# Local attention: sums of squares as four 64x64 tiles, rotation re-split between three engines, exponentials kept in PSUM

## The chip, the cores and the metric

The kernel runs on one core of one Trainium2 chip. The metric is the device time of one execution in microseconds. Before the change the median of two runs was 2688.89 us (2684.29 and 2693.5).

## What is computed

The reference is a stack of four layers on an input of 8 x 256 positions with 128 channels: additive attention, six blocks of local attention with a gated feed-forward part, a state-space layer, and a mixture of eight experts. The change touches only the second, which takes three quarters of the time. Per block, cut to what matters:

```
qkv = x @ Wqkv                                  # 16 heads of 64
q = q / max(norm(q), 1e-12) * q_scale           # norm over the 64 of a head
k = k / max(norm(k), 1e-12) * k_scale
q = q*cos*scale + rotate_half(q)*sin*scale      # rotary, per position
k = k*cos/scale + rotate_half(k)*sin/scale
sim = q . k over a window of 32 and the one before, * 8, masked
attn = softmax(sim);  out = attn @ v;  x = x + out @ Wo
x = x + (a * gelu(gate)) @ W2                   # (a, gate) = layernorm(x) @ W1
```

## The kernel before

`local_attention` (line 296 on) cuts the 2048 positions into four units of 512. Six layers of four units give 24 units, numbered i. Each unit has eight slots, j = 0 to 7, one for each pair of heads. The loop over the units 1 to 22 is a hardware loop (line 354); unit 0, unit 23 and the tail are written out. The order of the work on each engine is written out by hand, in a function `slot` per engine, and all engines meet through semaphores that count.

What slot j of unit i does is a pipeline. A pair of heads is projected in one slot, normalised in the next and scored in the one after:

- PE (TensorE), from line 528: scores of pair j (a mask by L449, then 32 small matmuls by L456), projection of q and k of pair j+2 (L429, L430, into PSUM banks 0 and 1), v of pair j+2 (L417, bank 2), the product of attention and v of pair j-2 (L477, bank 7), transposes of the probabilities of pair j-1 (L465, bank 6), and the sums of squares of pair j+2 (`norms`, L435 and L436, again into banks 0 and 1). `norms` multiplies 128 x 1024 squares by a 128 x 128 matrix that is block-diagonal, one 64 x 64 block of ones for each head of the pair.
- ACT (ScalarE), from line 642: a copy of the projection to SBUF (`f_raw`, L606), its square (L609), the exponential of the scores in place in SBUF (L662), copies of v (L598) and of the attention output (L634), three copies that spread the transposed probabilities (L624 to L627), and ln and exp for the inverse norm (L615, L617).
- POOL (GpSimd): `f_raw` times the cosine table (L707), then the sum of both halves of the rotation (L711).
- DVE (VectorE), from line 790: maximum and shift of the scores of pair j (L763, L767), normalisation of pair j+1 into `f_qk` (L755), the partition shuffle of `f_raw` of pair j+2 (L745), that times the sine table (L748), then the sum, the reciprocal and the scaling of the probabilities of pair j (L774, L776, L778).

The work behind the attention of unit i-1 is spread over the slots of unit i. On PE: `Wo` in slots 0 to 2 (L490, six, six and four passes), the mean of the layer norm in slot 3 (L497), its variance in slot 4 (L503), the gate and hidden matmuls in slots 5 to 7 (L510, L517), `W2` in slot 7 (L524). On DVE: the residual sum and `shift_in` of the new y into `f_xs2` at the end of slot 2 (L813, L724, L726), the centring at the end of slot 3 (L818, L821), the product with the inverse deviation at the end of slot 4 (L825), `shift_in` of the next unit's input at the end of slot 5, three `hidden` products (L786) in slots 6, 6 and 7. On ACT: square, ln and exp of the layer norm in slot 4 (L657, L676, L678), scale and bias in slot 5 (L667), three gelus with a table load before and after them (L639, L652) at the slots' border 5/6.

"Slot start" below is the start of L449, the mask of the scores. A float32 matmul appears as two records.

## Time and profile before

| | us |
|---|---|
| median of the runs shown | 2688.89 |
| the profiled execution, its own time | 2695.59 |
| its span in the profile | 2693.8 |
| PE busy | 2427.3 (90%) |
| DVE busy | 2276.3 (85%) |
| ACT busy | 1801.3 (67%) |
| POOL busy | 1082.1 (40%) |
| mean granted TensorE clock | 0.962 of 2.4 GHz |

The 192 slots of the local attention lie between 97 and 2150 us of the span. The time before them is additive attention; behind them come the state space and the experts, which the change leaves alone. A busy PE in the profile is not PE at its peak: records of matmuls overlap, so the pace of PE is read from the starts of successive groups.

### The profile page before, as it was taken

What the parts mean: (1) busy time and instruction counts of PE and PEld (TensorE: products, weight loads), DVE (VectorE), ACT (ScalarE), POOL (GpSimd) and SP (SyncE); (2) the same over time, 40 slices, a digit from 0 to 9 for tenths busy, and PEclk for the clock granted to TensorE, in tenths of its full rate; (3) what the DMA queues carried; (4) which work ended last, traced back from release to release, by engine and by line L of the source; (5) the groups of instructions that cost most, each with busy time, mean ns of one, the idle gap of its engine ahead of it and who ended that gap; (6) DMA issues with size and microseconds to landing.
All of it is one profiled execution on the core that took longest, in us unless ns stands there. A gap on an engine that the chain in (4) does not pass through costs nothing. (4 is left out here: it accounts for less than half of the span.)

```text
span 2693.8 us, 62735 instructions
## 1 busy us (share of the span) xinstructions
PE 2427.3 (90%) x24940; PEld 1267.8 (47%) x24940; DVE 2276.3 (85%) x2595; ACT 1801.3 (67%) x2593; POOL 1082.1 (40%) x461
## 2 busy tenths in 40 slices
PE   7899999999999999999999999999999977767778
PEld 2355555445555555455555555455545522222355
DVE  5799998998899998999889988998889848999542
ACT  4667776777677766777667766677677656545533
...
GB/s 20 53 2 2 2 25 10 10 2 1 14 22 10 2 2 13 14 18 1 2 14 14 15 5 2 13 14 9 10 2 2 2 36 0 0 0 0 18 16 47
DMA packets 16016, 29.85 MB, mean 11 GB/s; under 512 B 3616, under 2 KB 6064, under 8 KB 15664
## 3 DMA queue, kind: packets, MB, share of 16 engines
...
HBM read 24.73 MB, written 1.05 MB: 10 GB/s over the span
## 5 line engine op out<-in xcount | busy, mean ns | idle before, releaser
L707 POOL TENSOR_TENSOR f_rot<-f_raw,f_tabc 128x1024 f32<-128x1024 f32 x192 | 453.8, 2364 | 993.6 <-DVE f_qk L755 448.6
L711 POOL TENSOR_TENSOR f_rot<-f_rot,f_shuf 128x1024 f32<-128x1024 f32 x192 | 452.0, 2354 | 235.5 <-DVE f_shuf L748 235.5
L606 ACT ACTIVATE f_raw<-f_ps 128x1024 f32<-128x1024 f32 x192 | 196.1, 1021 | 348.6 <-PE f_ps L430 348.6
L748 DVE TENSOR_TENSOR f_shuf<-f_shuf,f_tabs 128x1024 f32<-128x1024 f32 x192 | 417.9, 2177 | 8.7
L778 DVE TENSOR_TENSOR f_s<-f_s,f_rcp 128x512 f32<-128x512 f32 x192 | 401.0, 2089 | 6.6
L477 PEld LDWEIGHTS f_ps<-f_ptz,f_v 64*64 64x64 f32 x6144 | 259.5, 133 | 96.0 <-issue 96.0
L477 PE MATMUL f_ps<-f_ptz,f_v 64*64 64x96 f32 (+1 forms) x6144 | 285.9, 243 | 1.9 <-ACT f_ptz L627 1.7
L429 PE MATMUL f_ps<-f_xs,f_wq 128*128 128x512 f32 x384 | 225.2, 670 | 46.9 <-DVE f_xs L726 34.6
L745 DVE STREAM_SHUFFLE f_shuf<-f_raw 128x1024 f32<-128x1024 f32 x192 | 257.7, 1342 | 0.6
L755 DVE SCALAR_TENSOR_TENSOR f_qk<-f_rn,f_rot 128x1024 f32<-128x1024 f32 x192 | 233.0, 1214 | 2.5 <-POOL f_rot L711 2.5
L456 PE MATMUL f_ps<-f_qk 64*32 64x64 f32 x12288 | 198.8, 220 | 34.8 <-issue 34.8
L615 ACT ACTIVATE f_rn<-f_ps 128x1024 f32<-128x1024 f32 x192 | 198.3, 1033 | 46.0 <-PE f_ps L436 45.6
L617 ACT ACTIVATE f_rn<-f_rn,k_lift 128x1024 f32<-128x1024 f32 x192 | 220.5, 1149 | 6.3
L417 PE MATMUL f_ps<-f_wv,f_xs 128*64 128x256 f32 x1536 | 216.3, 404 | 0.0
L430 PE MATMUL f_ps<-f_xs,f_wk 128*128 128x512 f32 x384 | 210.3, 631 | 0.0
L1133 POOL TENSOR_TENSOR s_prod<-s_state,s_cs 128x1024 f32<-128x1024 f32 x64 | 151.7, 2371 | 145.5 <-DVE s_state L1211 145.5
L609 ACT ACTIVATE f_sq<-f_raw 128x1024 f32<-128x1024 f32 x192 | 203.1, 1058 | 6.1
L435 PE MATMUL f_ps<-f_sq,f_same 128*128 128x512 f32 x384 | 197.7, 597 | 5.9 <-ACT f_sq L609 5.9
L456 PEld LDWEIGHTS f_ps<-f_qk 64*32 64x32 f32 x12288 | 163.5, 106 | 78.7 <-issue 78.7
L436 PE MATMUL f_ps<-f_sq,f_same 128*128 128x512 f32 x384 | 197.0, 595 | 0.0
L490 PE MATMUL f_ps<-f_o,f_wo 128*128 128x512 f32 x384 | 183.8, 612 | 0.0
L417 PEld LDWEIGHTS f_ps<-f_wv,f_xs 128*64 128x64 f32 x1536 | 96.1, 140 | 172.3 <-issue 144.1
...
## 6 DMA issues: line engine op xcount, KB each, us to landing
...
```

The lines of the kernel that those rows point to most:

```text
L417: mm = pe.matmul(view(ps, 2 * CH + 256 * r, [1, 256], p0=64 * h, rows=64), xs[:, at:at + 64], view(wv, CH * (q // 4) + 64 * h, [128, 4], [ ...
L429: pe.matmul(bank(0), wq[:, 128 * j:128 * j + 128], xs[:, :], start=True, stop=True)
L430: pe.matmul(bank(1), wk[:, 128 * j:128 * j + 128], xs[:, :], start=True, stop=True).then_inc(sem["a_mm"], 1)
L456: mm = pe.matmul(view(ps, (4 + h) * CH + (w // 4) * 64, [1, 64], p0=WIN * (w % 4), rows=WIN), t[64 * h:64 * h + 64, WIN * w:WIN * w + WIN] ...
L477: mm = pe.matmul(view(ps, 7 * CH + 64 * p, [1, n], p0=64 * h, rows=64), v[64 * h:64 * h + 64, p * CH + 64 * j:p * CH + 64 * j + 64], ptz[6 ...
L617: act.activation(rn[:, :], rn[:, :], ACT.Exp, scale=-0.5, bias=con.lift).then_inc(sem["rn"], 1)
L707: pool.tensor_tensor(view(rot, 0, [S, 4], [1, S]), view(raw, 0, [S, 4], [1, S]), view(tab_c, 0, [S, 2], [0, 2], [1, S]), ALU.mult).then_in ...
L711: pool.tensor_tensor(rot[:, :], rot[:, :], shuf[:, :], ALU.add).then_inc(sem["rot"], 1)
L745: dve.stream_shuffle(shuf[:, :], raw[:, :], [(p + 16) % 32 for p in range(32)]).then_inc(sem["shuf"], 1)
L748: dve.tensor_tensor(view(shuf, 0, [S, 4], [1, S]), view(shuf, 0, [S, 4], [1, S]), view(tab_s, 0, [S, 2], [0, 2], [1, S]), ALU.mult).then_i ...
L755: dve.scalar_tensor_tensor(out=view(qk[j % 2], 0, [KOFF, 2], [1, UNIT]), in0=view(rn, 0, [UNIT, 2], [1, UNIT]), scalar=1e12, in1=view(rot, ...
L778: dve.tensor_tensor(view(t, 0, [64, 8], [1, 64]), view(t, 0, [64, 8], [1, 64]), view(rc, 0, [1, 8], [0, 64]), ALU.mult).then_inc(sem["p"], 1)
```

## The change

Projection weights are rearranged on the host so that bank 0 holds q of the pair's first head in partitions 0 to 63 and k of the second head in 64 to 127, and bank 1 the other two. ACT no longer copies the projection to `f_raw`. It squares it straight from PSUM in four activations of 64 partitions, two of which write the squares of k to the other half of the partitions (`f_cross`). `norms` becomes four matmuls with a 64 x 64 matrix of ones, one for each quarter of the array, into banks 6 and 7 instead of 0 and 1. DVE shuffles the projection from PSUM and multiplies it, also from PSUM, with the cosine table; POOL now multiplies the shuffled copy with the sine table and adds. The exponentials are written to PSUM over the scores (banks 4 and 5), and the DVE sums and scales them from there. v moves to bank 6, the transposes to bank 2, the variance to bank 3, the first gate matmul to bank 6. SP's weight loads keep their order, in another loop.

In program order: ACT does the exponential of a slot ahead of the squares, where it came after `f_raw` and its square; DVE does shuffle and cosine product behind the scaling of the probabilities, where shuffle and sine product came ahead of it. `norms` waits for the squares, the copy of v and the copy of the attention output (`f_o`); scores wait for the scaled probabilities of the pair before (`f_p`) instead of for their shift.

```
-    GBANK = (2, 0, 1)
+    GBANK = (6, 0, 1)
+    NBANK = (6, 7)
 def project(i, j):                                   # PE
-    need(pe, sem["ln"], i * 8 + j)
+    need(pe, sem["sq"], i * 8 + j)
+    need(pe, sem["shuf"], i * 8 + j)
+    need(pe, sem["straight"], i * 8 + j)
 def norms(i, j):                                     # PE
-    need(pe, sem["sq"], i * 8 + j + 1)
-    pe.matmul(bank(0), same_head[:, :], sq[:, 0:UNIT], start=True, stop=True)
-    pe.matmul(bank(1), same_head[:, :], sq[:, UNIT:], start=True, stop=True).then_inc(sem["n_mm"], 1)
+    gather(sem["sq"], i * 8 + j + 1)
+    gather(sem["v"], i * 8 + j + 1)
+    gather(sem["o"], i * 8 + j - 3)
+    for own in (True, False):
+        for h in range(2):
+            k = slice(64 * h, 64 * h + 64)
+            of = sq[k, UNIT * h:UNIT * h + UNIT] if own else cross[k, :]
+            mm = pe.matmul(view(ps, NBANK[h] * CH, [1, CH], p0=64 * (h if own else 1 - h), rows=64),
+                           same_head[k, k], of, start=True, stop=True, skip_group_check=True)
+    mm.then_inc(sem["n_mm"], 1)
 def scores(i, j):                                    # PE
-    gather(sem["shift"], i * 8 + j)
+    gather(sem["p"], i * 8 + j)
 def square(i, j):                                    # ACT, for raw_copy
+    for own in (False, True):
+        for h in range(2):
+            k, other = slice(64 * h, 64 * h + 64), slice(64 * (1 - h), 64 * (1 - h) + 64)
+            to = sq[k, UNIT * h:UNIT * h + UNIT] if own else cross[other, :]
+            ins = act.activation(to, view(ps, (h if own else 1 - h) * CH, [1, CH], p0=64 * h, rows=64), ACT.Square)
+    ins.then_inc(sem["sq"], 1)
 def rotate(i, j):                                    # POOL
+    pool.tensor_tensor(shuf, shuf, tab_s, ALU.mult).then_inc(sem["turned"], 1)
     pool.tensor_tensor(rot[:, :], rot[:, :], shuf[:, :], ALU.add).then_inc(sem["rot"], 1)
 def shuffle(i, j):                                   # DVE
+    need(dve, sem["sq"], i * 8 + j + 1)
+    dve.stream_shuffle(shuf[:, :], view(ps, 0, [1, 2 * CH]), [(p + 16) % 32 for p in range(32)])
 def straight(i, j):                                  # DVE
+    dve.tensor_tensor(rot, ps banks 0 and 1, tab_c, ALU.mult).then_inc(sem["straight"], 1)
 def soft_b(i, j):                                    # DVE
-    dve.tensor_tensor(s, s, rc, ALU.mult)            # all three in SBUF
+    dve.tensor_tensor(s, ps banks 4 and 5, rc, ALU.mult)
 def gate_mm / hid_mm: hid_mm(k, 0) now comes ahead of gate_mm(k, 0), which waits for "ln" of the slot
```

ACT in slot 5 of the looped unit. Before (`f_cen`, `f_xn` and the second `f_sq` belong to the layer norm of the unit before):

```order
L678 ACTIVATE f_sq<-f_sq 128x512 [waits f_ln2]
L292 REGISTER_ALU
L606 ACTIVATE f_raw<-f_ps 128x1024 [waits f_straight,f_shuf,f_a_mm]
L609 ACTIVATE f_sq<-f_raw 128x1024 [waits f_n_mm,f_raw]
L598 ACTIVATE f_v<-f_ps 128x2x256 [waits f_v_mm]
L662 ACTIVATE f_s<-f_s 128x512 [waits f_shift]
L667 ACTIVATE f_xn<-f_xn,f_fcol 128x512 [waits f_scaled]
L634 ACTIVATE f_o<-f_ps 128x512 [waits f_pv_mm]
```

and now:

```order
L722 ACTIVATE f_sq<-f_sq 128x512 [waits f_ln2]
L700 ACTIVATE f_ps<-f_s 128x2x256 [waits f_shift]
L292 REGISTER_ALU
L652 ACTIVATE f_cross<-f_ps 64x512 [waits f_n_mm,f_a_mm]
L652 ACTIVATE f_cross<-f_ps 64x512
L652 ACTIVATE f_sq<-f_ps 64x512 x2
L641 ACTIVATE f_v<-f_ps 128x2x256 [waits f_v_mm]
L711 ACTIVATE f_xn<-f_xn,f_fcol 128x512 [waits f_scaled]
L679 ACTIVATE f_o<-f_ps 128x512 [waits f_pv_mm]
```

The exponential (`f_s`, waiting for `f_shift`) has moved from behind the squares to ahead of them.

PE from the transposes of slot 5 to the scores of slot 6. Before:

```order
L465 MATMUL f_ps<-f_ident,f_s 128x128 x3
L292 REGISTER_ALU
L435 MATMUL f_ps<-f_sq,f_same 128x512 [waits f_sq]
L436 MATMUL f_ps<-f_sq,f_same 128x512
L510 MATMUL f_ps<-f_xn,f_w 128x512 [waits f_w1,f_xn,f_v]
L517 MATMUL f_ps<-f_xn,f_w 128x512
L449 MATMUL f_ps<-f_maskb,f_identb 128x256 [waits f_qk,f_shift]
```

and now:

```order
L507 MATMUL f_ps<-f_ident,f_s 128x128 x3
L435 REGISTER_ALU
L475 MATMUL f_ps<-f_sq,f_same 64x512 [waits f_sq,f_v,f_o]
L475 MATMUL f_ps<-f_sq,f_same 64x512
L475 MATMUL f_ps<-f_cross,f_same 64x512 x2
L558 MATMUL f_ps<-f_xn,f_w 128x512 [waits f_w1,f_xn]
L548 MATMUL f_ps<-f_xn,f_w 128x512 [waits f_ln]
L490 MATMUL f_ps<-f_maskb,f_identb 128x256 [waits f_qk,f_p]
```

The sums of squares wait for two more results, the gate matmul for the ln that reads them, and the scores for the scaled probabilities.

DVE around the end of slot 4. Before:

```order
L755 SCALAR_TENSOR_TENSOR f_qk<-f_rn,f_rot 128x2x512 [waits f_rn,f_rot]
L292 REGISTER_ALU
L745 STREAM_SHUFFLE f_shuf<-f_raw 128x1024 [waits f_raw,f_rot]
L748 TENSOR_TENSOR f_shuf<-f_shuf,f_tabs 128x1024 [waits f_tab,f_shuf]
L774 TENSOR_REDUCE f_sum<-f_s 128x8 [waits f_exp]
L776 RECIPROCAL f_rcp<-f_sum 128x8 [waits f_sum]
L778 TENSOR_TENSOR f_s<-f_s,f_rcp 128x512 [waits f_rcp]
L825 TENSOR_TENSOR f_xn<-f_cen,f_sq 128x512 [waits f_fcol,f_rs2]
L763 TENSOR_REDUCE f_max<-f_ps 128x8 [waits f_s_mm]
```

and now:

```order
L802 SCALAR_TENSOR_TENSOR f_qk<-f_rn,f_rot 128x2x512 [waits f_rn,f_rot]
L822 TENSOR_REDUCE f_sum<-f_ps 128x8 [waits f_exp]
L825 RECIPROCAL f_rcp<-f_sum 128x8 [waits f_sum]
L827 TENSOR_TENSOR f_s<-f_ps,f_rcp 128x2x4x64 [waits f_rcp]
L292 REGISTER_ALU
L788 STREAM_SHUFFLE f_shuf<-f_ps 128x1024 [waits f_sq,f_rot]
L795 TENSOR_TENSOR f_rot<-f_ps,f_tabc 128x1024 [waits f_qk,f_tab,f_sq]
L875 TENSOR_TENSOR f_xn<-f_cen,f_sq 128x512 [waits f_fcol,f_rs2]
L811 TENSOR_REDUCE f_max<-f_ps 128x8 [waits f_s_mm]
```

The product into `f_xn` stays last in the slot and ahead of the next slot's maximum; in front of it stand now the shuffle and the cosine product, which read PSUM, and the shuffle waits for the squares.

## Rows read from the trace of the kernel before

**Rows 1.** Timeline of PE, slot 3: start us, us, operation, xcount
```profile
1238.82 0.38 PE L449 MATMUL f_ps<-f_maskb,f_identb 128*128 128x256 bf16 x2
...
1242.08 1.08 PE L417 MATMUL f_ps<-f_wv,f_xs 128*64 128x256 f32 x8
1243.09 1.49 PE L477 MATMUL f_ps<-f_ptz,f_v 64*64 64x96 f32 x32
1244.51 1.13 PE L497 MATMUL f_ps<-f_xs,k_ones 128*128 128x512 f32 x2
...
1245.91 1.02 PE L435 MATMUL f_ps<-f_sq,f_same 128*128 128x512 f32 x2
...
1247.63 0.38 PE L449 MATMUL f_ps<-f_maskb,f_identb 128*128 128x256 bf16 x2
```

**Rows 2.** Timeline of PE, slots 5 to 0: idle time before in brackets
```profile
1256.85 0.38 PE L449 MATMUL f_ps<-f_maskb,f_identb 128*128 128x256 bf16 x2
...
1265.89 1.10 PE L510 MATMUL f_ps<-f_xn,f_w 128*128 128x512 f32 x2 [0.84 <-issue]
...
1267.68 0.38 PE L449 MATMUL f_ps<-f_maskb,f_identb 128*128 128x256 bf16 x2
...
1273.52 1.12 PE L429 MATMUL f_ps<-f_xs,f_wq 128*128 128x512 f32 x2 [1.20 <-DVE f_xs L726]
...
1279.56 0.38 PE L449 MATMUL f_ps<-f_maskb,f_identb 128*128 128x256 bf16 x2
...
1291.40 0.38 PE L449 MATMUL f_ps<-f_maskb,f_identb 128*128 128x256 bf16 x2 [0.43 <-issue]
...
1294.60 0.64 PE L456 MATMUL f_ps<-f_qk 64*32 64x64 f32 x11 [2.04 <-issue]
```

**Rows 3.** Windows: most of the stage, two slots 0; length, engines' busy times, PEclk
```profile
130.00:2130.00 2000.00, 1890.83 (x22806) 1023.99 (x22806) 1812.51 (x2087) 1438.26 (x2088) 878.12 (x373) 0.98 0.03 9
1206.32:1218.80 12.48, 10.72 (x125) 5.85 (x126) 12.09 (x14) 5.17 (x9) 6.83 (x3) 1.00 0.06 18
1291.40:1306.85 15.45, 13.41 (x124) 6.78 (x125) 12.83 (x14) 5.20 (x9) 7.06 (x3) 0.78 0.01 2
```

**Rows 4.** Timeline of DVE and POOL, slots 3 and 4
```profile
1243.48 0.69 DVE L763 TENSOR_REDUCE f_max<-f_ps 128x8 f32<-128x512 f32 x1
...
1244.82 1.22 DVE L755 SCALAR_TENSOR_TENSOR f_qk<-f_rn,f_rot 128x1024 f32<-128x1024 f32 x1
...
1245.96 1.33 DVE L745 STREAM_SHUFFLE f_shuf<-f_raw 128x1024 f32<-128x1024 f32 x1
1246.20 2.36 POOL L707 TENSOR_TENSOR f_rot<-f_raw,f_tabc 128x1024 f32<-128x1024 f32 x1 [4.86 <-DVE f_qk L755]
...
1247.32 2.33 DVE L748 TENSOR_TENSOR f_shuf<-f_shuf,f_tabs 128x1024 f32<-128x1024 f32 x1
...
1249.79 2.35 POOL L711 TENSOR_TENSOR f_rot<-f_rot,f_shuf 128x1024 f32<-128x1024 f32 x1 [1.23 <-DVE f_shuf L748]
...
1250.52 2.18 DVE L778 TENSOR_TENSOR f_s<-f_s,f_rcp 128x512 f32<-128x512 f32 x1
```

**Rows 5.** The line of `shift_in`: durations ns min/median/max, first and last start us, forms
```profile
L724 DVE TENSOR_SCALAR f_xs<-y_t x48: 407/416/421, 80.4 to 2159.9; 64x512 f32 x44, 64x512 f32<-64x512 f32 x4
```

**Rows 6.** Timeline of ACT, slots 3 to 5
```profile
1242.19 1.02 ACT L606 ACTIVATE f_raw<-f_ps 128x1024 f32<-128x1024 f32 x1 [0.96 <-PE f_ps L430]
...
1245.47 0.58 ACT L598 ACTIVATE f_v<-f_ps 128x512 f32<-128x512 f32 x1
1245.95 0.59 ACT L634 ACTIVATE f_o<-f_ps 128x512 f32<-128x512 f32 x1
...
1257.16 1.05 ACT L615 ACTIVATE f_rn<-f_ps 128x1024 f32<-128x1024 f32 x1
...
1260.00 0.63 ACT L678 ACTIVATE f_sq<-f_sq 128x512 f32<-128x512 f32 x1
1260.54 1.00 ACT L606 ACTIVATE f_raw<-f_ps 128x1024 f32<-128x1024 f32 x1
...
1264.46 0.63 ACT L662 ACTIVATE f_s<-f_s 128x512 f32<-128x512 f32 x1 [1.34 <-DVE f_s L767]
```

More of the change, by code:

```diff
@@ L321, in local_attention @@
         v = m.sb("f_v", 8 * CH)
[L322 to L324 removed]
+        sq, shuf, rot = (m.sb(f"f_{n}", 2 * UNIT) for n in ("sq", "shuf", "rot"))
+        rn, cross = m.sb("f_rn", 2 * UNIT), m.sb("f_cross", UNIT)
+        AT = (WIN, 2 * WIN + UNIT)
+        qk = [m.sb(f"f_qk{b}", AT[1] + UNIT) for b in range(2)]
         s = [m.sb(f"f_s{b}", UNIT) for b in range(2)]
@@ L378, in weights, with load_w1, load_w2, layer @@
             sp.dma_start(wo[:, :], io["f_wo"][r]).then_inc(sem["wo"], 16)
-            need(sp, sem["h_mm"], t * 3)
+        def load_w1(sp, r, t):
+            gather(sp, sem["h_mm"], t * 3)
             sp.dma_start(w1[:, :], io["f_w1"][r]).then_inc(sem["w1"], 16)
-            need(sp, sem["w2_mm"], t)
+        def load_w2(sp, r, t):
+            gather(sp, sem["w2_mm"], t)
             sp.dma_start(w2[:, :], io["f_w2"][r]).then_inc(sem["w2"], 16)
+        def layer(sp, r, first, last):
+            for q in range(8 * NU):
+                if not first and q == 4:
+                    load_wo(sp, r, r * NU)
+                if not first and q == 9:
+                    load_w1(sp, r, r * NU)
+                if not first and q == 10:
+                    load_w2(sp, r, r * NU)
+                if not last and q == 8 * NU - 5:
+                    load_qkv(sp, r + 1, (r + 1) * NU, 0)
+                if not last and q == 8 * NU - 1:
+                    load_qkv(sp, r + 1, (r + 1) * NU, 1)
@@ L392, in _ @@
             load(sp, sem["const"], consts)
-            weights(sp, 0, 0)
-            with sp.Fori(1, DEPTH) as r:
-                weights(sp, r, r * NU)
+            for k in range(2):
+                load_qkv(sp, 0, 0, k)
+            load_wo(sp, 0, 0)
+            load_w1(sp, 0, 0)
+            load_w2(sp, 0, 0)
+            layer(sp, 0, True, False)
+            with sp.Fori(1, DEPTH - 1) as r:
+                layer(sp, r, False, False)
+            layer(sp, DEPTH - 1, False, True)
         @block.tensor
@@ L652, in slot @@
                     nc.scalar.preload_act_table_set(ACT_SET)
+                if run:
+                    need(act, sem["shift"], i * 8 + j + 1)
+                    act.activation(view(ps, 4 * CH, [CH, 2], [64, 4], [1, 64]), view(s[j % 2], 0, [64, 2], [128, 4], [1, 64]),
+                                   ACT.Exp, scale=8.0).then_inc(sem["exp"], 1)
                 if has:
-                    raw_copy(u, a)
+                    square(u, a)
                 if before and j == 4:
@@ L657, in slot @@
                     act.activation(sq2[:, :], cen[:, :], ACT.Square).then_inc(sem["sq2"], 1)
-                if has and j == 5:
-                    value_copy(u, a)
-                if run:
-                    need(act, sem["shift"], i * 8 + j + 1)
-                    act.activation(s[j % 2][:, :], s[j % 2][:, :], ACT.Exp, scale=8.0).then_inc(sem["exp"], 1)
-                if has and j != 5:
+                if has:
                     value_copy(u, a)
@@ L675, in slot @@
                     need(act, sem["var"], k + 1)
-                    act.activation(sq2[:, :], bank(2), ACT.Ln, bias=con.eps).then_inc(sem["ln2"], 1)
+                    act.activation(sq2[:, :], bank(3), ACT.Ln, bias=con.eps).then_inc(sem["ln2"], 1)
                     need(act, sem["ln2"], k + 1)
@@ L810, in slot @@
                     soft_b(i, j)
+                if has:
+                    shuffle(u, a)
+                    straight(u, a)
                 if before and j == 2:
```

134 lines of the change are left out of this document (71 added, 63 removed).

## Prediction

> **What bounds the kernel now.** I read the shares of busy time first, then the starts of groups on PE through one unit, then what PE waited for, and then DVE, POOL and ACT in the same stretch. The starts on PE show one slot of local attention as a closed row of groups: slot 3 goes from 1238.82 to 1247.63, 8.81 us, with no idle time given [rows 1]. The sums of squares take 1247.63 - 1245.91 = 1.72 us of it, four records of 0.43 us. Slot 5 takes 10.83 us, slot 6 11.88, slot 7 11.84, and in these PE waits 0.84, 1.20 and 0.43 us [rows 2]. Slot 0 takes 12.48 us at full clock and 15.45 where the granted clock is 0.78 (a part of it at 1.2 instead of 2.4 GHz), and PE stands idle for 2.04 us inside the scores [rows 2, 3]. So PE sets the pace with few waits, some 86 us per unit.
>
> DVE is nearly as full, but part of its time is standing behind POOL. The product L748 begins at 1247.32 and ends at 1249.65, that is 1.09 us after POOL's L707 ended (1246.20 + 2.36 = 1248.56). L778 begins at 1250.52 and ends at 1252.70, 0.56 us after L711 ended (1252.14). Both read two tensors from SBUF, as POOL does. The shuffle L745, with one, takes its 1.33 us right beside L707 [rows 4].
>
> **The change, part by part.** I count in microseconds from the slot's start, and price slots 0 to 7 of a looped unit.
>
> PE, sums of squares. Before, two 128x128 matmuls of 512 columns, 1.72 us. Now four 64x64 tiles. v's matmuls (128x64, two tiles) bring eight records of 256 columns, 0.215 each in sequence, 1.72 together, into 1243.09 - 1242.08 = 1.01 us [rows 1]: two tiles run beside each other (0.86) and the change of array shape costs 0.15. If all four tiles run together the new sums cost two passes of 0.43, plus about 0.25 for two changes of shape: 1.1 us, 0.62 less. If only two do, it is 1.72 + 0.25, 0.25 more. Tiles that share rows do overlap in v's rows, so I take four: -0.62 wherever PE alone sets the slot.
>
> DVE. The sine product (2.33) becomes a cosine product from PSUM. The nearest row, the shift, is 512 columns from PSUM in 0.69, so some 1.2 for 1024; the scaling (2.18) becomes 0.7. That frees 2.6 us a slot, but of the chain to `f_qk` nothing gets shorter. POOL now starts only behind the shuffle and does both of its operations in a row. The cycle is shuffle 1.36, POOL 2.36 + 2.35 with 0.2 of semaphores, normalisation 1.14, sum to scaling 1.6: 9.0 us [rows 4]. That is under the mean slot of 10.6 ((1291.40 - 1206.32) / 8 [rows 2, 3]), above PE's new slot 3; it hides over the unit as a whole.
>
> ACT. Copy and square (2.1 us) become four activations of 64 partitions; 512 columns follow each other at 1245.95 - 1245.47 = 0.48 [rows 6], so 1.95. Nothing gained. But the exponential now stands ahead of them, and `norms` waits for the copy of the attention output, which is third behind them. That is a new chain: DVE's shift of slot j, exponential (0.65), squares (1.95), v (0.5), output (0.6), sums of squares on PE. Before, the squares started 1242.19 - 1238.82 = 3.37 into the slot whatever DVE did [rows 6]. Where the shift ends 2.7 into the slot, as without extra work on DVE, the sums start at 6.6 instead of 6.1. Where it is late, PE now waits for it.
>
> Slots 0 and 1: six `Wo` passes (2.6) cover the new wait. -0.6 each. Slot 2: the squares start 1.8 later, behind `Wo`; sums at 8.15 against 7.9: -0.4.
>
> Slot 3: DVE's shuffle of slot 2 started at 7.0. Behind it come the cosine product, the residual sum and three instructions of `shift_in`. These used to run with POOL idle; now POOL's product runs until 10.8. One bound is that they are not held: shift of slot 3 ends at 3.3, PE does slot 3 in 8.2 (-0.6). The other is that they are held as L748 and L778 are, and again by the sum behind it: DVE is free 5.0 into slot 3, shift 6.3, squares until 8.9, sums at 9.95, slot 11.0 (+2.2). No row shows this kind beside POOL; its 512 columns take 0.416 [rows 5], faster than the 0.69 of every form that runs undisturbed, so I take it as held once: shift ends at 3.9, slot 8.5, -0.3.
>
> Slot 4: the centring, behind the cosine product, ends about 3.6 into the slot, the shift at 5.0, squares 7.6, the layer norm's own square, v and output 9.15, sums until 10.1, variance: 11.1 instead of 9.23, +1.9 (9.5 with nothing held, 10.1 in a long slot 3).
>
> Slot 5: the inverse deviation comes from ACT behind ln and exp of the norm. That sequence took from 1257.16 to 1260.63, 3.47 us [rows 6]; it now starts when slot 4's sums are done, and ends 2.7 into slot 5. DVE then does `f_xn`, two tensors from SBUF with POOL's sum running: held, like L778, until about 3.9. Shift 5.2, exponential 5.9, squares 7.9, v, `f_xn`'s bias 0.75, output: 9.6; sums until 10.6; then the first hidden matmul, and the gate matmul behind the ln: 13.2 instead of 10.83, +2.4. Before, the exponential stood just as late (1264.46, 7.6 into the slot) and it hurt nothing, because raw copy and square had gone first (1260.54) [rows 2, 6]. Even with nothing held I get 12.75, +1.9. This is the surest loss.
>
> Slot 6: `f_xs` comes earlier, PE's 1.20 goes; next is `hidden`, now ahead of the scaling that the scores wait for: 11.1, -0.7. Slot 7: -0.4, with a wait of 0.3 for the output copy.
>
> Sum of a unit: -0.6 - 0.6 - 0.4 - 0.3 + 1.9 + 2.4 - 0.7 - 0.4 = +1.3, to which the clock comes. The mean clock of 0.98 [rows 3] means 4% of the time, 3.5 us per unit, at 1.2 GHz, and it follows idle time of some 2.5 us around slot 0. In slot 0, (1 - 0.78) x 2 x 15.45 = 6.8 us at half clock cost 15.45 - 12.48 = 3.0, 0.44 per us. The new waits of PE (3 in slot 4, 3.5 in slot 5) are as long as that. With as much half clock once more per unit, 3.5 x 0.44 = 1.5. Zero and 4 are the ends.
>
> So +2.8 per unit, for 23 units, and nothing for unit 0, which has no feed-forward work: +64. On the profiled execution's 2695.6 (span 2693.8) that is 2760; the median shown is 6.7 lower, so 2753. SP's weight loads keep their order and conditions: 0.
>
> On the port the Trainium skill (SBUF — State Buffer, section on the two sides of SBUF) says that DVE operations in a 2-port mode or with two SBUF inputs and GpSimd's operations exclude each other for a whole instruction. Rows 4 agree for two inputs. By that rule `shift_in` is held as well, which is the long slot 3 below.
>
> **The rivals.** (a) *Held twice.* POOL's sum gets the port between two instructions of `shift_in`. Slots 3, 4, 5 are 11.0, 10.1, 12.95: +5.2 instead of +4.0. With a clock loss of up to 4: +6.5 x 23 = +150 at worst, about 2805 with middle values. For it: the two holds in rows 4. Against: DVE may keep its turn.
> (b) *Nothing held but `f_xn`, clock unchanged.* Slots 3 to 5 come to 31.8 against 28.9, +2.9, the others -2.7: +0.2, 2695.
> (c) *PE's saving stands: faster.* The place is the start of the sums in slot 5, the price 0.62 a slot. If they start before 7.0, and in slot 4 before 7.2, the waits are covered: -0.6 in each of slots 0, 1, 3 and 4, -0.4 in 2 and 7, -0.7 in 6, 0 in 5, together -3.9 x 23 = -90, so 2600. For it: DVE really loses 2.6 us a slot, and with the cover of slot 0 everything could run earlier than my chain says. Against: the 3.47 us on ACT are no shorter.
> (d) *Tiles run two by two.* +0.87 in the PE-bound slots 0, 1, 2, 7: +3.5 more per unit, 2830.
>
> On tiles that share a bank the Trainium skill (TensorEngine Tiling (Array Packing), Gotcha 1) says that different row tiles can't write the same PSUM bank at once. Here each row half writes its own bank, 6 or 7. The rule speaks for four at a time, as the sum has it.
>
> **How the numbers follow.** The forecast 0.42, (a) 0.20, (b) 0.18, (c) 0.15, (d) 0.05. A measurement here can tell about 2%, 54 us, from no change: slower is above 2743. The forecast lies just above, so I give 0.25 of its 0.42 to slower and 0.17 to the same. Slower 0.50, same 0.35, faster 0.15. The range goes from 2635, inside the gap to (c), to 2835.
>
> **What would show it.** Right: in the rows of PE, slots 4 and 5 longer than 9.23 and 10.83 with idle time ahead of the sums, named after `f_o`; the sums taking 1.0 to 1.2 us; DVE's products at 1.2 and 0.7 us; DVE busy far less and idle behind POOL; a product into `f_xn` of over 0.7 us; the granted clock below 0.98. Wrong: sums in slot 5 starting right behind the transposes, slots of 10.2 or less there, or half-clock stretches around slot 0 alone.

## The result and the profile after

The changed kernel takes 2788.86 us (median of two runs, 2788.75 and 2788.98) against 2688.89. The ratio is 1.037, 95% interval 1.033 to 1.041: slower. The profiled execution took 2788.98 us with a span of 2787.2, and that is 93.4 us more than the span of before. The forecast was 2753 and slower.

The busy times first. This is part 1 of the page, and two rows of its part 5 (busy, mean ns of one, then the idle time ahead of them and who ended it):

```profile
PE 2354.2 (84%) x25708; PEld 1190.9 (43%) x25708; DVE 1980.3 (71%) x2597; ACT 1898.5 (68%) x2977; POOL 1081.4 (39%) x461
...
L475 PE MATMUL f_ps<-f_sq,f_same 64*64 64x512 f32 x768 | 218.6, 641 | 264.6 <-ACT f_o L679 255.6
...
L802 DVE SCALAR_TENSOR_TENSOR f_qk<-f_rn,f_rot 128x1024 f32<-128x1024 f32 x192 | 233.9, 1218 | 70.4 <-POOL f_rot L754 70.0
```

PE has 73 us less to do and DVE 296 us less, and yet the kernel is longer: PE now stands for 264.6 us ahead of the sums of squares, nearly all of it for the copy of the attention output, `f_o`. The timeline of PE shows where. These are the sums at the end of slot 0, then slots 3 to 7 and the next slot 0, in the looped unit that begins at 1174 (start us, us, idle time in brackets; L490 is the mask that starts a slot, L475 the sums of squares):

```profile
1183.23 0.65 PE L475 MATMUL f_ps<-f_sq,f_same 64*64 64x512 f32 x2
...
1183.72 0.60 PE L475 MATMUL f_ps<-f_cross,f_same 64*64 64x512 f32 x2
1184.25 0.39 PE L490 MATMUL f_ps<-f_maskb,f_identb 128*128 128x256 bf16 x2
...
1203.73 0.39 PE L490 MATMUL f_ps<-f_maskb,f_identb 128*128 128x256 bf16 x2
...
1214.02 0.65 PE L475 MATMUL f_ps<-f_sq,f_same 64*64 64x512 f32 x2 [3.13 <-ACT f_o L679]
...
1215.04 0.39 PE L490 MATMUL f_ps<-f_maskb,f_identb 128*128 128x256 bf16 x2
...
1223.63 0.65 PE L475 MATMUL f_ps<-f_sq,f_same 64*64 64x512 f32 x2 [2.34 <-ACT f_o L679]
...
1225.61 0.38 PE L490 MATMUL f_ps<-f_maskb,f_identb 128*128 128x256 bf16 x2
...
1235.28 0.65 PE L475 MATMUL f_ps<-f_sq,f_same 64*64 64x512 f32 x2 [3.43 <-ACT f_o L679]
...
1236.30 2.08 PE L558 MATMUL f_ps<-f_xn,f_w 128*128 128x512 f32 x2
1238.17 1.80 PE L548 MATMUL f_ps<-f_xn,f_w 128*128 128x512 f32 x2
1239.81 0.38 PE L490 MATMUL f_ps<-f_maskb,f_identb 128*128 128x256 bf16 x2
...
1251.07 0.39 PE L490 MATMUL f_ps<-f_maskb,f_identb 128*128 128x256 bf16 x2
1259.06 0.65 PE L475 MATMUL f_ps<-f_sq,f_same 64*64 64x512 f32 x2 [0.82 <-ACT f_o L679]
1263.69 0.38 PE L490 MATMUL f_ps<-f_maskb,f_identb 128*128 128x256 bf16 x2 [0.77 <-issue]
...
1273.73 0.39 PE L490 MATMUL f_ps<-f_maskb,f_identb 128*128 128x256 bf16 x2
```

The rows of the four tiles start 0.49 us apart, and the scores' mask follows after 1184.25 - 1183.23 = 1.02 us, where it followed 1.72 us after the start of two full ones [rows 1]. So the tiles do what they should. But slot 3 is 11.31 us (8.81 in rows 1), slot 4 10.57, slot 5 14.20 (10.83 in rows 2). The slots of all looped units, from the starts of the scores' mask, as medians over 22 units:

| slot | 0 | 1 | 2 | 3 | 4 | 5 | 6 | 7 | mean unit |
|---|---|---|---|---|---|---|---|---|---|
| before | 14.0 | 10.5 | 9.5 | 8.8 | 9.2 | 10.8 | 11.8 | 11.9 | 86.4 |
| after | 10.0 | 9.8 | 9.7 | 11.3 | 11.0 | 14.2 | 11.3 | 12.3 | 89.9 |

Of the 93.4 us, 78 lie in the 22 looped units (3.55 each). Unit 0 is 3.2 us longer and unit 23, up to its last slot, 6.2, and the first slot starts at 105.1 us instead of 98.1, though nothing ahead of it was meant to change; why it does was not looked into. The windows that answer to [rows 3], the same stretch and slots 3, 4, 5 and 0 of the unit above (length, busy PE, PEld, DVE, ACT, POOL, granted clock, DMA share, GB/s):

```profile
130.00:2130.00 2000.00, 1739.87 (x22657) 908.85 (x22656) 1467.76 (x2005) 1470.81 (x2361) 843.62 (x358) 0.96 0.03 8
...
1203.73:1215.04 11.31, 8.18 (x128) 4.49 (x125) 10.57 (x14) 7.20 (x12) 4.71 (x3) 1.00 0.01 1
1215.04:1225.61 10.57, 8.23 (x128) 4.51 (x125) 8.62 (x12) 8.66 (x14) 6.31 (x3) 1.00 0.01 2
1225.61:1239.81 14.20, 10.77 (x128) 5.38 (x127) 10.88 (x12) 11.60 (x18) 7.16 (x4) 0.88 0.01 1
...
1263.69:1273.73 10.04, 9.85 (x129) 5.21 (x129) 7.12 (x11) 4.99 (x11) 5.69 (x3) 1.00 0.09 23
```

The clock of 0.96 instead of 0.98 means about (1 - 0.96) x 2 x 2000 = 160 us at 1.2 GHz instead of 80. Per looped unit the clock records give 7.0 us at 1.2 GHz instead of 3.6. Before, all of it lay in slot 0; now there is none there, and 2.9 lie in slot 4 and 3.6 in slot 5. In the unit above the clock fell after idle stretches of 3.13, 2.34 and 3.43 us, and the two feed-forward groups at the end of slot 5 take 1.87 and 1.64 us in place of about 0.9 each [rows 2]. Slot 0, on the other hand, has lost its stop: 10.04 us at full clock, against 12.48 and 15.45 [rows 3].

Why the sums come late in slot 3 is seen on DVE, POOL and ACT from the end of slot 2 to the end of slot 3; this answers to [rows 4, 6]:

```profile
1202.86 1.21 DVE L795 TENSOR_TENSOR f_rot<-f_ps,f_tabc 128x1024 f32<-128x1024 f32 x1
...
1204.70 0.99 DVE L767 TENSOR_SCALAR f_xs<-y_t 64x512 f32 x1
1205.70 2.56 DVE L769 TENSOR_SCALAR f_xs<-y_t 64x255 f32 x2
...
1209.02 0.69 DVE L815 TENSOR_TENSOR f_s<-f_ps,f_max 128x512 f32<-128x512 f32 x1
...
1211.71 0.69 DVE L827 TENSOR_TENSOR f_s<-f_ps,f_rcp 128x512 f32<-128x512 f32 x1
```

```profile
1203.04 2.36 POOL L750 TENSOR_TENSOR f_shuf<-f_shuf,f_tabs 128x1024 f32<-128x1024 f32 x1 [6.25 <-DVE f_shuf L788]
1205.55 2.35 POOL L754 TENSOR_TENSOR f_rot<-f_rot,f_shuf 128x1024 f32<-128x1024 f32 x1
```

```profile
1209.74 0.60 ACT L700 ACTIVATE f_ps<-f_s 128x512 f32<-128x512 f32 x1 [3.67 <-DVE f_s L815]
1210.37 1.19 ACT L652 ACTIVATE f_cross<-f_ps 64x512 f32<-64x512 f32 x2
1211.57 1.19 ACT L652 ACTIVATE f_sq<-f_ps 64x512 f32<-64x512 f32 x2
1212.79 0.60 ACT L641 ACTIVATE f_v<-f_ps 128x512 f32<-128x512 f32 x1
1213.28 0.59 ACT L679 ACTIVATE f_o<-f_ps 128x512 f32<-128x512 f32 x1
```

Read it from below. PE's sums start at 1214.02, when `f_o` is written; it is behind v, the four squares (2.4 us) and the exponential, and ACT stood idle for 3.67 us because DVE's shift ended at 1209.71. DVE was in `shift_in`: its first copy, 0.41 to 0.42 us when undisturbed [rows 5], ends at 1205.69 behind POOL's product (ends 1205.40), the second pair takes 2.56 us and ends at 1208.26 behind POOL's sum (ends 1207.90).

### The profile page after: what moved, and what is told of

Read it like the earlier page. It is cut to its first block and busy times, and to the rows that moved or that the text cites. A ratio compares the mean times of both kernels' runs of the same rounds, so it can differ in the third digit from the quotient of the medians.

```text
span 2787.2 us, 65659 instructions
## 1 busy us (share of the span) xinstructions
PE 2354.2 (84%) x25708; PEld 1190.9 (43%) x25708; DVE 1980.3 (71%) x2597; ACT 1898.5 (68%) x2977; POOL 1081.4 (39%) x461
## 5 line engine op out<-in xcount | busy, mean ns | idle before, releaser
L750 POOL TENSOR_TENSOR f_shuf<-f_shuf,f_tabs 128x1024 f32<-128x1024 f32 x192 | 452.6, 2357 | 1293.0 <-DVE f_shuf L788 1293.0
L475 PE MATMUL f_ps<-f_sq,f_same 64*64 64x512 f32 x768 | 218.6, 641 | 264.6 <-ACT f_o L679 255.6
L700 ACT ACTIVATE f_ps<-f_s 128x512 f32<-128x512 f32 x192 | 115.6, 602 | 279.6 <-DVE f_s L815 279.4
L652 ACT ACTIVATE f_cross<-f_ps 64x512 f32<-64x512 f32 x384 | 226.9, 591 | 91.7 <-PE f_ps L464 86.4
L788 DVE STREAM_SHUFFLE f_shuf<-f_ps 128x1024 f32<-128x1024 f32 x192 | 249.9, 1302 | 0.9
L811 DVE TENSOR_REDUCE f_max<-f_ps 128x8 f32<-128x512 f32 x192 | 131.9, 687 | 154.8 <-PE f_ps L498 153.3
L795 DVE TENSOR_TENSOR f_rot<-f_ps,f_tabc 128x1024 f32<-128x1024 f32 x192 | 231.5, 1206 | 0.0
L652 ACT ACTIVATE f_sq<-f_ps 64x512 f32<-64x512 f32 x384 | 227.0, 591 | 4.5
L475 PE MATMUL f_ps<-f_cross,f_same 64*64 64x512 f32 x768 | 218.8, 648 | 0.0
L449 PE MATMUL f_ps<-f_wv,f_xs 128*64 128x256 f32 x1536 | 210.4, 395 | 1.2 <-ACT f_rn L659 1.2
```

Source lines behind the costliest of these rows:

```text
L449: mm = pe.matmul(view(ps, 6 * CH + 256 * r, [1, 256], p0=64 * h, rows=64), xs[:, at:at + 64], view(wv, CH * (q // 4) + 64 * h, [128, 4], [ ...
L475: mm = pe.matmul(view(ps, NBANK[h] * CH, [1, CH], p0=64 * (h if own else 1 - h), rows=64), same_head[k, k], of, start=True, stop=True, ski ...
L652: ins = act.activation(to, view(ps, (h if own else 1 - h) * CH, [1, CH], p0=64 * h, rows=64), ACT.Square)
L750: pool.tensor_tensor(view(shuf, 0, [S, 4], [1, S]), view(shuf, 0, [S, 4], [1, S]), view(tab_s, 0, [S, 2], [0, 2], [1, S]), ALU.mult).then_ ...
L788: dve.stream_shuffle(shuf[:, :], view(ps, 0, [1, 2 * CH]), [(p + 16) % 32 for p in range(32)]).then_inc(sem["shuf"], 1)
L795: dve.tensor_tensor(view(rot, 0, [S, 4], [1, S]), view(ps, 0, [S, 4], [1, S]), view(tab_c, 0, [S, 2], [0, 2], [1, S]), ALU.mult).then_inc( ...
```

## The experiments

The first six start from the changed kernel, the last four from the kernel before. The ratio is to the kernel before, measured beside each; a gain is counted from the changed kernel's 2788.86 us. "Slots" are medians as in the table, and times into a slot are medians over the looped units too.

**1. Undoing the order of ScalarE in slots 3 to 5.**

```
-                if run:
+                if run and j not in (3, 4, 5):
                     (exponential, ahead of the squares)
+                if run and j in (3, 4, 5):
+                    (the same, behind the copy to f_o)
```

> The changed kernel, with the exponential of slots 3, 4 and 5 moved behind squares, copy of v and output copy on ACT. Theory, the new wait of the sums is the exponential ahead of the squares: the sums start 7 us into the slot whatever DVE does; slots 3, 4, 5 go from 11.3, 11.0, 14.1 to about 9, 9.4, 11.3, together 7 us per unit, about 2630 us. Rival, DVE's lateness itself sets the slot, because the scores wait for the scaled probabilities that come out of the same chain: the three slots lose under 2 us together, 2745 or more.

Measured: 2720.35 us, ratio 1.010 (1.006 to 1.014), between the two expectations. Slots 3 to 7: 9.1, 10.8, 12.0, 12.4, 12.3. Of the 98 us that separate the changed kernel from the kernel before (2690.41 beside this run), 68 go. Slots 3 and 5 lose 2.2 us each, slot 4 little and slot 6 gets longer by 1.1. The PE rows of slot 4 show what comes in its place:

```profile
1087.13 0.38 PE L490 MATMUL f_ps<-f_maskb,f_identb 128*128 128x256 bf16 x2 [0.93 <-DVE f_s L831]
1089.47 1.10 PE L463 MATMUL f_ps<-f_xs,f_wq 128*128 128x512 f32 x2 [1.04 <-DVE f_rot L799]
1095.78 0.65 PE L475 MATMUL f_ps<-f_sq,f_same 64*64 64x512 f32 x2 [1.33 <-ACT f_o L679]
```

The late exponential makes the scaled probabilities and the rotation late, and the scores and the projection of the next slot wait for them.

**2. The product with the inverse deviation one slot later on DVE, behind the maximum and shift of slot 5.**

```
                 if run:
                     soft_a(i, j)
+                if before and j == 5:
+                    need(dve, sem["rs2"], k + 1)
+                    need(dve, sem["fcol"], k + 1)
+                    dve.tensor_tensor(xn[:, :], cen[:, :], sq2[:, :], ALU.mult)...
-                if before and j == 4:      (the same, at the end of slot 4)
```

> The changed kernel, with the product into f_xn moved on DVE from the end of slot 4 to behind maximum and shift of slot 5. Theory, the wait for the inverse deviation (f_rs2) delays the shift of slot 5 and with it all on ACT: the shift of slot 5 ends at 2.7 instead of 4.4 us, the sums start at about 7.3 instead of 9.7, slot 5 falls from 14.1 to about 11; 3 us per unit, about 2720 us. Rival, the gate matmul's wait for ln or the half clock sets slot 5: it loses under 1 us, 2765 or more.

Measured: 2720.26 us, ratio 1.010 (1.007 to 1.014). Slot 5 falls from 14.2 to 11.0, no other by more than 0.2; slot 3 rises by 0.4. A hit. The wait of DVE for ACT's ln and exp stood ahead of the shift of slot 5, and with it the whole chain. In the changed kernel the row is:

```profile
1228.25 0.69 DVE L875 TENSOR_TENSOR f_xn<-f_cen,f_sq 128x512 f32<-128x512 f32 x1 [3.89 <-ACT f_sq L722]
```

Of the 3.2 us, 1.9 are sums that start earlier (7.8 us into the slot instead of 9.7); the other 1.3 are the end of the slot, which has no half clock any more.

**3. `shift_in` and the copy to `f_fcol` with the factor 1 read from a column in SBUF instead of a constant.**

```
-  dve.tensor_scalar(to[0:64, :], y[...], 1.0, None, ALU.mult)
+  dve.tensor_scalar(to[0:64, :], y[...], one[0:64, 0:1], None, ALU.mult)      (and the three others)
```

> The changed kernel, with the 1.0 of shift_in and of the copy into f_fcol read from a column of ones instead of given as a constant (L736 in the kernel before has that form and takes 1.35 ns per element, longer than shift_in's 0.8). Theory, held at the port: this form waits for nobody on POOL; the three instructions take 0.6 + 0.35 + 0.35 instead of 0.99 + 2.56 us, f_fcol 0.15 instead of 1.45. Slot 3 falls from 11.3 to about 8.8 us, slot 4 from 11.0 to about 10.3; 3.3 us per unit, about 2713 us. Rival, the sums of squares are late for another reason (the order on ACT alone): shift_in gets shorter and slots 3 and 4 lose under 0.5 us each, 2770 or more.

Measured: 2804.08 us, 1.040 (1.036 to 1.044). A miss: this form is held all the same, and slot 3 is 11.7.

```profile
1208.18 0.99 DVE L768 TENSOR_SCALAR f_xs<-y_t,f_one 64x512 f32 x1
1209.18 2.62 DVE L770 TENSOR_SCALAR f_xs<-y_t,f_one 64x255 f32 x2
```

So it says nothing on what the hold costs. Edits 2 and 3 together:

> Both edits of the two runs before: plain form of shift_in, product into f_xn behind the shift of slot 5. Theory, two separate delays: the gains add, about 6.3 us per unit, 2645 us, below the kernel before. Rival, one takes the place of the other: no faster than the better of the two alone.

2718.07 us, 1.009 (1.006 to 1.012), slots 3 to 5 11.9, 11.1, 11.0: edit 2 alone, within 3 us.

**4. The same copies as the larger of a value and itself, two operands in SBUF.**

```
-  dve.tensor_scalar(to[0:64, :], y[...], 1.0, None, ALU.mult)
+  dve.tensor_tensor(to[0:64, :], y[...], y[...], ALU.max)                    (and the three others)
```

> The changed kernel, with the copies of shift_in and of f_fcol written as products of two operands in SBUF (the larger of a value and itself) in place of a multiplication by a number: the form of f_xn's product, which the trace doesn't show held by POOL. Theory (the hold by POOL delays DVE's shift of slot 3, behind it the exponential, the squares and PE's sums): the three copies take about 0.5, 0.5 and 0.2 us instead of 0.99, 2.56 and 1.45; slot 3 falls from 11.3 to 8.8 to 9.3 us, slot 4 from 11.0 to 10.3 or stays, slot 5 keeps its 14.1; 23 times about 3 us: 2715 to 2735 us. Rival (slot 3 is long because the exponential stands ahead of the squares, and the hold only comes in its shadow): slot 3 stays above 10.5 us, 2770 to 2790 us.

Measured: 2813.17 us, 1.045 (1.043 to 1.048). Both expectations missed, but the miss is worth more than a hit:

```profile
1213.83 1.25 DVE L767 TENSOR_TENSOR f_xs<-y_t 64x512 f32 x1
1215.10 2.82 DVE L769 TENSOR_TENSOR f_xs<-y_t 64x255 f32 x2
```

The copies are held too and take 0.5 us longer (4.07 in place of 3.55 us), and slot 3 is 12.4 instead of 11.3, 1.1 more where DVE shows 0.5. A longer hold makes a longer slot 3: PE's sums start 10.8 us into it instead of 10.3. Most of the rest is the clock: the sums themselves take 1.5 us instead of 1.1, and slot 3 has 1.2 us at half clock on average, where the changed kernel has 0.35. With edit 2 on top:

> The changed kernel with both edits: the copies in the two-operand form, and f_xn's product behind soft_a of slot 5. If the two losses are separate, slots 3, 4, 5 are about 9.1, 10.5 and 11.0 us (they were 11.3, 11.0, 14.1), and the time is that of the later product alone, 2720 us, less what the form gives by itself, 55 to 75 us: 2645 to 2665 us, below the kernel before. If they share one wait (PE late in slot 3 also makes slot 5 late), less than the sum: 2680 to 2720 us.

2735.84 us, 1.018 (1.015 to 1.020), slots 3 to 5 12.7, 11.1, 11.0: 77 us less than with the copies alone. Both ranges missed, since the shorter slot 3 that they counted on did not come. The later product is worth 69 us on the changed kernel, 86 on the copies of edit 3 and 77 here, and slot 5 comes to 11.0 each time, however long slot 3 is; the two losses are separate.

**5. `f_xs` formed from PSUM.** The three instructions add y and the bank of the output projection themselves, ahead of y's own sum:

```
-  dve.tensor_tensor(ycol, ycol, bank(3), ALU.add)
-  need(dve, sem["y1"], k + 1)
-  shift_in(xs2, k % NU, sem["xs2"])
-  need(pe, sem["xs2"], i + 1)                (ahead of the mean's matmul)
+  need(pe, sem["y1"], i + 1)
+  dve.tensor_tensor(xs2[0:64, :], y[0:64, ...], bank(3)[0:64, :], ALU.add)
+  for b in range(2):
+      mm = dve.tensor_tensor(xs2[64:128, ...], y[64:128, ...], bank(3)[64:128, ...], ALU.add)
+  mm.then_inc(sem["xs2"], 1)
+  need(dve, sem["xs2"], k + 1)
+  dve.tensor_tensor(ycol, ycol, bank(3), ALU.add)
```

> The changed kernel, with f_xs for the mean formed at slot 2 straight from y and the bank of the output projection (three sums with one operand in PSUM, 64x512 and twice 64x255) ahead of y's own sum, in place of copies from y behind it; f_fcol's copy is as it was. Theory (what is held by POOL is an operation with no operand in PSUM; the hold is what makes slot 3 long): the three operations take about 0.7 and twice 0.4 us, 1.5 in place of 3.6; DVE's shift, ACT's exponential and squares and PE's sums of slot 3 come 2.0 us earlier; slot 3 is 9.0 to 9.5 us (11.3), slot 4 10.3 to 11.0, slot 5 unchanged at 14.1: 2735 to 2750 us. The kernel whose copies were 0.5 us longer had a slot 3 that was 1.0 us longer, which speaks for it. Rival (the operations are held all the same, 3.5 us together): 2785 to 2795 us.

Measured: 2708.13 us, 1.006 (1.004 to 1.007). DVE at the end of slot 2:

```profile
1073.63 0.67 DVE L863 TENSOR_TENSOR f_xs<-y_t,f_ps 64x512 f32<-64x512 f32 x1
1074.31 0.76 DVE L865 TENSOR_TENSOR f_xs<-y_t,f_ps 64x255 f32<-64x255 f32 x2
```

0.67 and 0.76 us while POOL's product runs (from 1072.69, for 2.37 us): not held. The shift of slot 3 ends 3.75 us into the slot instead of 5.97, and slot 3 is 9.1. That is the mechanism as expected; the gain of 81 us is more than the 40 to 55 expected, because slot 5 falls too, to 12.0, while slot 4 rises to 11.7. In slot 5 the inverse deviation comes 0.9 us earlier (1.70 us into the slot instead of 2.60), and the sums with it. The other 1.2 us come at the end of the slot, and the clock records have less half clock there, 1.9 us on average instead of 3.6. Why the clock fell less was not isolated.

**6. Edits 5 and 2 and the exponential late in slot 3 alone**, the attempt to beat both kernels:

> The changed kernel with three edits: f_xs formed from PSUM at slot 2, f_xn's product behind soft_a of slot 5, and the exponential of slot 3 alone behind the output copy. Sum of what each did or should do: slots 3, 4, 5 about 8.9, 10.3 and 11.0 us where they were 11.3, 11.0 and 14.1, 6.2 us less in each of 23 units: 2640 to 2660 us, below the kernel before and level with the padded kernel before. If the exponential ahead of the squares in slots 4, 6 and 7 sets the rest of the loss, slot 4 stays at 11 to 12 us: 2660 to 2690 us.

Measured: 2705.37 us, 1.004 (1.002 to 1.006): both ranges missed. Slots 3 to 5 are 9.1, 12.8 and 11.0. The gains do not add: the late exponential (in three slots), the later product and the copies from PSUM are worth 68, 69 and 81 us alone, and this combination 83. PE's waits over the whole kernel:

```profile
L463 PE MATMUL f_ps<-f_xs,f_wq 128*128 128x512 f32 x384 | 225.6, 671 | 38.0 <-DVE f_rot L799 27.0 <-DVE f_xs L773 7.9 <-issue 0.2
L475 PE MATMUL f_ps<-f_sq,f_same 64*64 64x512 f32 x768 | 212.5, 626 | 166.5 <-ACT f_o L679 157.1 <-ACT f_v L641 9.4
L490 PE MATMUL f_ps<-f_maskb,f_identb 128*128 128x256 bf16 x384 | 76.2, 281 | 35.1 <-DVE f_s L831 24.8 <-issue 10.3
```

The wait ahead of the sums is down from 264.6 to 166.5 us, but PE now waits 52 us for DVE ahead of the projection (`f_rot`) and of the scores (`f_s`). In slot 4 the shift now ends 5.5 us into the slot (3.6 in the changed kernel). In experiment 5, with the same short slot 3, it is 3.6 as well; here DVE's sum of slot 3 waited 1.9 us for the late exponential, and all of DVE's work behind it is late. Whether edits 5 and 2 without it beat the kernel before is open; they were not tried.

**7. The order alone, on the kernel before**: the exponential ahead of the copy of q and k, in all slots.

```
+                if run:
+                    need(act, sem["shift"], i * 8 + j + 1)
+                    act.activation(s, s, ACT.Exp, scale=8.0)        (ahead of raw_copy)
-                if run:  (the same, behind it)
```

> The kernel before with the order of ScalarE's work alone changed as the change does: the exponential ahead of the copy of q and k and of their squares, in all slots; tiles, copies and exponentials stay as they are. Theory (the exponential waits for DVE's shift, and the squares and PE's sums behind it wait with it; so the order alone costs in the slots where DVE is late): slots 3, 4 and 5 each longer by 1 to 2.5 us, slots 0, 1, 2 by less than 0.5: 2750 to 2850 us. Rival (the exponential ahead is harmless, the losses come from the tiles and PSUM): within 0.7% of 2690 us.

Measured: 2759.86 us, 1.025 (1.022 to 1.028). Slots 3 to 7: 10.6, 11.0, 11.4, 10.6, 12.2; slots 1 and 2 as before; slot 0 is shorter (12.3 instead of 14.0), and so is slot 6 (10.6 instead of 11.8), so that the 67 us are what is left after these gains. A hit in the total, with a smaller step in slot 5 (0.6 us). One line of PE tells it, beside 5.9 us of idle time in this place before:

```profile
L435 PE MATMUL f_ps<-f_sq,f_same 128*128 128x512 f32 x384 | 207.3, 622 | 137.7 <-ACT f_sq L609 137.5
```

So the order alone turns a covered lateness of DVE into a wait of PE, with no tile and no PSUM changed.

**8. Exponentials in PSUM alone, on the kernel before**: exponential to PSUM, sum and scaling from there, and the next scores wait for the scaled probabilities.

```
-  gather(sem["shift"], i * 8 + j)
+  gather(sem["p"], i * 8 + j)
-  act.activation(s, s, ACT.Exp, scale=8.0)
+  act.activation(ps banks 4 and 5, s, ACT.Exp, scale=8.0)       (soft_b reads there)
```

> The kernel before with the third part of the change alone: the exponential writes to PSUM, the sum and the product of soft_b read it there, and the next scores wait for that product. Theory (the later release of the scores' banks is covered, and the products from PSUM are about as long): all slots within 0.3 us of before, 2675 to 2705 us. Rival (the later release delays the scores): each of slots 1 to 7 longer by 0.3 us and more, 2740 us and more. Rival (the exponential in PSUM frees DVE from the hold by POOL and brings the saving of the changed kernel's slots 0 to 2 by itself): 2650 us and less.

Measured: 2913.44 us, 1.083 (1.081 to 1.086): the first rival, though unevenly. Slots 1 and 5 are as before, slots 2, 6 and 7 longer by 1.7, 1.8 and 5.1 us. The scaling is down to 0.69 us as it should be, but the scores wait:

```profile
L449 PE MATMUL f_ps<-f_maskb,f_identb 128*128 128x256 bf16 x384 | 82.2, 300 | 226.9 <-DVE f_s L780 226.7
```

In this kernel the scaling is the last of a slot's DVE work, behind shuffle and sine product, and the banks come free only then. The changed kernel has the same wait and stands 2.1 us in it (its scores' row has 11.7 us of idle time, 2.1 of it for `f_s`), and shuffle and product are behind the scaling there. That the two parts of the change need each other is read from these two orders; no run has the new order of DVE alone.

**9. Sums of squares as two pairs of tiles on the diagonal, on the kernel before.**

```
-  pe.matmul(bank(0), same_head[:, :], sq[:, 0:UNIT], ...)            (and bank 1)
+  for b in range(2):
+      for h in range(2):
+          k = slice(64 * h, 64 * h + 64)
+          pe.matmul(view(ps, b * CH, ..., p0=64 * h, rows=64), same_head[k, k], sq[k, UNIT * b:...], ...)
```

> The kernel before with its sums of squares as four matmuls of 64x64 tiles instead of two of 128x128, on the same squares: the tiles of q together, those of k behind them, each pair on the diagonal of the array. Theory (tiles in different rows and columns of the array run together, and all four are needed to halve the time): the four matmuls take 1.75 to 1.95 us (1.72 before), no slot is shorter, and the change of mode costs 0.1 us: 2685 to 2715 us, nearer the upper end. Rival (a 64x64 tile takes less than a full one by itself): under 1.5 us, 2660 us and less. Rival (tiles of one pair run one after the other): 3.4 us, above 2950 us.

Measured: 2728.29 us, 1.013 (1.011 to 1.017), above the range. The sums:

```profile
1099.73 1.93 PE L438 MATMUL f_ps<-f_sq,f_same 64*64 64x512 f32 x8
1101.60 1.13 PE L507 MATMUL f_ps<-f_sq,k_ones 128*128 128x512 f32 x2
```

The next group follows after 1101.60 - 1099.73 = 1.87 us: two pairs take as long as two full matmuls (1.72), plus 0.15. So the 1.02 us needs all four quarters at once. Slots 1 to 3 are 0.2 us longer each, slots 4 and 5, where PE waits, 0.2 shorter; of the mean unit's 1.5 us more, most is in slot 0 (15.4 us), where the stop of experiment 10 lies. PE has more instructions in each slot here, and the stop has moved: it comes after 8 of slot 0's 64 small matmuls, not after 53, and is longer.

**10. The kernel before with 125 instructions more on PE, outside its loop.**

```
             (iterations, ahead of the hardware loop)
+            for _ in range(pad):
+                eng.sem_inc(sem["seen"], 1)
-            iterations(pe, slot, behind)
+            iterations(pe, slot, behind, 125)
```

> The kernel before with 125 increments of an unused semaphore on PE ahead of its loop, nothing else. The kernel before stands still for 1.8 to 2 us inside the scores of slot 0, after 53 matmuls, with nothing to wait for but a transfer of instructions; the changed kernel doesn't. If that stop belongs to where the loop's start falls in the blocks in which instructions are fetched, the padding moves or removes it: slot 0 goes from 13.9 to between 10 and 12 us, the time to 2600 to 2645 us. If it belongs to the loop itself (a jump back costs it wherever it stands), slot 0 stays near 13.9 and the time within 0.5% of 2690 us.

Measured: 2643.94 us, 0.983 (0.981 to 0.986), as the first expectation has it and the fastest kernel of this study. Nothing inside the loop has changed. First a slot 0 of the kernel before, then one of the padded kernel:

```profile
1206.32 0.38 PE L449 MATMUL f_ps<-f_maskb,f_identb 128*128 128x256 bf16 x2 [0.45 <-issue]
1206.63 0.85 PE L456 MATMUL f_ps<-f_qk 64*32 64x64 f32 x53
1209.23 0.41 PE L456 MATMUL f_ps<-f_qk 64*32 64x64 f32 x11 [1.76 <-issue]
```

```profile
1107.92 0.38 PE L451 MATMUL f_ps<-f_maskb,f_identb 128*128 128x256 bf16 x2
1108.23 0.99 PE L458 MATMUL f_ps<-f_qk 64*32 64x64 f32 x64
```

The padding has a price of its own, paid once, where it stands between unit 0 and the loop:

```profile
192.72 0.58 PE L451 MATMUL f_ps<-f_maskb,f_identb 128*128 128x256 bf16 x2 [17.72 <-issue]
```

In the kernel before the stop comes after 53 of the 64 matmuls in each of units 2 to 22 (the slot 0 of [rows 2] shows the other 11) and not in units 0, 1 and 23: once after each jump back of the loop, always at the same instruction. In experiment 7 it is at 53 too, in experiment 9 at 8. With the padding it is gone, slot 0 is 10.5 or 10.6 us in each of units 2 to 22 and the clock of 130 to 2130 us is 0.99. A looped unit is 3.3 us shorter (83.1 instead of 86.4), 73 us over the loop; the 17.7 and smaller differences outside the loop leave 54 of them between the profiled executions and 46 between the medians. The changed kernel has other code ahead of and in its loop and has lost the stop as well.

The traces say more of what the stop waits for. In experiments 7 and 9 and in the kernel before, a transfer on the queue of instructions ends 0.7 to 1.8 us into each of these slots 0, and PE goes on 1.2 to 1.6 us after that end in all 63 cases: the later the transfer, the longer the stop. In experiment 8 PE's instructions are as many as in the kernel before, and yet there is no stop: PE stands 2.6 us ahead of this slot waiting for `f_s`, and the transfer ends 0.3 to 1.3 us before the slot begins. In the padded and in the changed kernel the transfer ends 1.1 to 1.8 us into the slot, as before, and PE does not wait for it. That speaks for a wait for instructions, which PE meets only where the code lies so, and only if it comes early enough. Which of the two spares the changed kernel its stop is open.

## Why the prediction was right, and where it was not

The total came out as said: slower, 2789 us inside 2635 to 2835 (forecast 2753), with the largest loss in slot 5, which it had named as the surest. It was right for part of the steps; that the sum came as near is luck, since its two largest errors, slots 0 and 3, cancel. Per looped unit:

| slot | forecast | measured | what the runs say |
|---|---|---|---|
| 0 | -0.6 | -4.0 | the stop inside the scores went, 3.5; not foreseen |
| 1 | -0.6 | -0.7 | four tiles at once |
| 2 | -0.4 | +0.2 | PE waits 0.7 us for `f_o` |
| 3 | -0.3 | +2.5 | `shift_in` held twice, rival (a) |
| 4 | +1.9 | +1.8 | as forecast |
| 5 | +2.4 | +3.3 | as forecast, plus half clock |
| 6 | -0.7 | -0.5 | near the forecast, though PE now waits 1.2 us for `f_o` |
| 7 | -0.4 | +0.5 | waits of 0.82 (`f_o`) and 0.77 us |
| clock | +1.5 | in the slots | 3.4 us more at half clock, forecast 3.5 |
| sum | +2.8 | +3.55 | from the mean units; the medians above add up to 3.0 |

**Outside the loop.** Unit 0 was put at nothing and the time ahead of the stage was given no cost; they took 3.2 and 7.1 us more. Unit 23, priced at 2.8 like the looped ones, took 6.2.

**The tiles.** "1.1 us, 0.62 less" is confirmed at 1.02, and experiment 9 confirms the reason: in pairs there is nothing to gain.

**DVE.** The cosine product takes 1.21 and the scaling 0.69 us, where 1.2 and 0.7 were said. DVE waits 70.0 us for POOL's sum, as said, on average 1.3 us in slot 0, 0.5 in slots 1 and 4 and nothing in the others. "It hides over the unit as a whole" holds: slots 0 and 1 are no longer for it, and in slots 3 and 5, where most is lost, DVE does not stand for this sum.

**The chain on ScalarE.** "A new chain: DVE's shift, exponential, squares, v, output, sums" was the core, and it is shown three times: experiment 7 makes it without the rest of the change and pays 67 us, experiment 1 breaks it in three slots and gains 68, and PE's wait is named after `f_o`. One of its terms was too small: the four squares take 2.4 us (1210.37 to 1212.76), not 1.95. That was read from 512 columns on 128 partitions overlapping at 0.48 us; these follow each other at 0.6. The 0.45 us account for most of slot 2.

**Slot 3 is the step that failed.** The forecast had `shift_in` "held once", with the shift of slot 3 ending at 3.9 us and a slot of 8.5. It is held twice, as in rival (a), whose price, shift at 6.3 us and a slot of 11.0, was nearly exact (6.0 and 11.3). Experiment 4 lengthens the hold and slot 3 with it, experiment 5 removes it and slot 3 is 9.1. The forecast rested on the short undisturbed time of the form, 0.416 us, but that the form is fast did not mean that it gets past POOL's second instruction. By the rule on the port pair the Trainium skill (SBUF — State Buffer, section on the two sides of SBUF) had `shift_in` held, and the trace agrees: 0.99 and 2.56 us, each ending just behind one of POOL's instructions.

**Slot 5.** The output copy ended 9.5 us into the slot; 9.6 was said. The product into `f_xn` began at 1228.25 when ACT's exp had ended at 1228.22 and POOL's sum at 1228.21, and took 0.69 us, so no hold can be read from it; "held until about 3.9" was wrong at 3.3, and ACT's 0.45 us made up for it. Experiment 2 shows that the place of the product is the cause. The slot's further 1.0 us is the half clock in its last two groups, which stood in the forecast as a term of its own.

**Slot 0 is the larger miss.** The forecast took the 2.04 us of idle time in it for part of the kernel. It was a stop that depends on where the code lies (experiment 10). Against the padded kernel slot 0 is only 0.5 us shorter (10.0 and 10.5), about the 0.6 that the tiles were to give. Against it the whole change costs 1.0368 / 0.9832 = 1.0545, about 145 us, and 6.85 us per looped unit (89.9 and 83.1). Rival (a) at its worst, 5.2 - 2.7 + 4 = +6.5, is nearer to that than the forecast.

**Rivals.** (b), nothing held but `f_xn`, fell with slot 3; its sum was wrong too, for by the forecast's own terms slots 3 to 5 are 8.2 + 9.5 + 13.2 = 30.9, not 31.8, which makes it 0.7 per unit less than before instead of 0.2 more. (c), PE's saving stands, asked for sums of slot 5 at 7.0 us; they came at 9.7. (d), tiles two by two, is out.
